# A new order of the small work around the scan steps of a Mamba layer: places by half step, delta and its product by channel half

## The chip, the cores and the metric

The kernel runs on one core of one Trainium2 chip. The metric is the device time of one execution in microseconds, the median of several runs. Work is spread over TensorE (PE), VectorE (DVE), ScalarE (ACT), GpSimd (POOL) and the DMA queue that SyncE (SP) feeds.

## The reference

An input of 4 x 128 x 128 x 128 (batch, channels, height, width) passes two layers. Layer 0 is a Mamba block over windows of 8 x 8 pixels:

```
tn  = layernorm over channels of the window's 64 tokens
xi, z = tn @ W_in                  (256 channels each)
xc  = silu(causal conv of xi over 4 taps + conv_b)
dr, Bm, Cm = xc @ W_x              (8, 16, 16 columns)
delta = softplus(dr @ dt_w + dt_b)
h_t = exp(delta_t * A) * h_(t-1) + (delta_t * xc_t) * B_t      for 16 states
y   = sum over states of h * C + xc * D,   then y * silu(z)
out = y @ W_out + b_out + x
```

Layer 1 normalises over channels, multiplies 16 filters in the frequency domain, mixes channels, applies a two-layer perceptron and adds its input. The change does not touch layer 1.

## The kernel before

**Blocks and steps.** Layer 0 is cut into 64 blocks of 16 windows (1024 tokens). A block is 32 steps (NSTEP): step n scans state n % 16 for half of the tokens (n < 16 the first 512, then the others), on all 256 channels held as 128 partitions x 2 halves. Every engine has one instruction stream, and `body(S, p)` of each engine writes it out step by step. `slots` runs the bodies: while block m is scanned (S.scan), the same 32 steps carry the front of block m+1 (S.front: projections, convolution, silu, delta), the layer norm of block m+2 (S.ahead), the output projection of block m-1 (S.back) and its spectra (S.tail). The engines are coupled by semaphores alone.

**One scan step.** In an even step (DSTEPS) the decay exp(delta*A) is written by ScalarE into the one PSUM buffer decay_d (`make_decay`, L734), and the drive delta*x*B is made by GpSimd (`make_drive`, L1020) from b_all, a row of B spread over the partitions by a DMA. In an odd step (RSTEPS) the decay goes to one of two SBUF buffers decay_r (L734), and the drive is made on ScalarE in token order (`scale_u`, L747, from ut and bt) and turned by TensorE into the one PSUM buffer drive_r (`turn_drive`, L591: 8 transposes). VectorE scans (L911, 32 a block). The product with C is made either by GpSimd (BY_GPSIMD: 20 of the 32 steps, L1031, with c_all from a DMA) or by VectorE (the 12 others, L922, with C spread by TensorE into PSUM, `broadcast_c`, L582). Three steps later TensorE adds the product into y_acc (`add_state`, L604: 8 transposes). Rings: 4 states, 4 products, 4 drives, 4 b_all, 4 c_all, one decay_d, one drive_r.

**Small work.** All other matrix work is a list of jobs, JOBS: (step, name, kind, bank). They share two PSUM banks, job_bank[0] and [1]; bank 0 also takes `broadcast_c`. A job waits until the job before it in its bank was read ("taken"), and a job in bank 0 waits also for the products of VectorE of all earlier steps. The names: z00 to z11 and conv00 to conv11 (channel half, token half), xp (the rows dr, B, C), dt (delta), bt and ut (B and delta*x turned to token order), turn (y turned back), out, mean, var, fy. The table AT says in which step the reader takes each result: `take_z` and `take_conv` (L771), `take_rows` (L754, L755), `take_dt`, `softplus`, `silu` and `copy_y` (L820) on ScalarE, `take_low` (L940), `take_ut` (L945), `gate` (L951), x1 (L967), stats (L973), mean_var (L977) on VectorE, `add_soft` (L1038), `make_du` (L1044), tn (L1069), edge (L1074) on GpSimd. A step has one place for this work on each engine: before `add_state` on TensorE, at the end of the step on the others. A convolution is already two half jobs, one step apart. `silu` costs two loads of activation tables besides its two activations.

**SyncE.** Its stream issues the loads of b_all 8 steps and of c_all 6 steps ahead, each after a wait on GpSimd that the buffer is free (L518, L524), and the loads and stores of x_in, x_res, x1 and the row spectra z (L566). All run on one queue in program order, and a wait holds back all that is behind it.

Of the kernel before, what the change touches and what calls it, by code (L numbers as in the profile page):

```python
# [63 lines left out]
BY_GPSIMD = tuple(sorted(RSTEPS + (2, 14, 18, 30)))  # L64
# [4 lines left out]

JOBS = [  # L70
# [14 lines left out]
]  # L85
SKIP_AT = {4: 0, 6: 1, 13: 2, 15: 3, 19: 0, 23: 1, 27: 2, 31: 3}
ADD_FIRST = (2, 18)
# [3 lines left out]
    "copy_y": (18, 2), "take_rows": (17, 0), "take_conv": (3, 8, 10, 12), "take_z": (0, 2, 8, 14),  # L91
# [2 lines left out]

# [2 lines left out]

# [1 line left out]

    "x_in": 15, "rows": (18, 1), "rows_landed": (24, 8), "x1_out": 18, "x_res": 23, "yo_out": 30,  # L100
}

# [28 lines left out]
class Slot:  # L131
# [14 lines left out]
    def at(self, n):  # L146
        return [j[1] for j in self.mine if j[0] == n]

    def jobs_below(self, bank, n):
        return self.start[bank] + sum(j[3] == bank and j[0] < n for j in self.mine)  # L150
# [263 lines left out]
def layer0(nc, a, wt, rows_dram, x1_dram, y_dram, blocks):  # L414
    with ExitStack() as ctx:
# [87 lines left out]
        def _(sp):  # L503
# [28 lines left out]
            def body(S, p):  # L532
# [3 lines left out]
                for n in range(NSTEP):  # L536
# [10 lines left out]
                    for k in range(NSTEP):  # L547
                        if k in DSTEPS and (k - B_LOAD) % NSTEP == n and S.step(n + B_LOAD, p):
                            load_b(S.step(n + B_LOAD, p))
                        if k in BY_GPSIMD and (k - C_LOAD) % NSTEP == n and S.step(n + C_LOAD, p):  # L550
                            load_c(S.step(n + C_LOAD, p))
                    if n == AT["x_in"] and S.ahead:
                        if S.front:
                            full(sp, S, "z11")
                        load_x(x_in, after, s["x_ready"])
                    if n == AT["x1_out"] and S.back:
                        need(sp, s["stats_done"], m)
                        sp.dma_start(x1_dram[bass.ds((m - 1) * WS, WS)].rearrange("r w c -> w r c"),
                                     x1[:]).then_inc(s["x1_stored"], 16)
# [4 lines left out]
                    if n == AT["yo_out"] and S.tail:  # L564
                        need(sp, s["yo_done"], m - 1)
                        sp.dma_start(yv[bass.ds(behind[1], 1), bass.ds(behind[0], 1)]  # L566
                                     .rearrange("o q f r d -> (o q f) r d"), yo[:]).then_inc(s["yo_stored"], 16)
# [8 lines left out]
        def _(pe):  # L576
            def broadcast_c(S, step):
# [3 lines left out]
                need(pe, job_taken[0], S.jobs_below(0, n + 1))  # L581
# [33 lines left out]
            def job(S, p, n, name, part=0):  # L615
# [50 lines left out]
                elif kind == "ut":  # L666
                    h, q = int(name[-2]), int(name[-1])
                    need(pe, s["du_done"], (m if q else m + 1) * 2 + q + 1)
                    for g in range(2):
                        for hf in range(2):  # L670
                            mm = pe.matmul(misc[:, (g * 2 + hf) * P:(g * 2 + hf + 1) * P],
                                           du[:, hf, q * HT + (2 * h + g) * P:q * HT + (2 * h + g + 1) * P],
                                           wt["ident"][:], start=True, stop=True, is_transpose=True)
# [19 lines left out]
                elif kind == "fy":  # L693
                    q = int(name[-1])
                    need(pe, s["z1_done"], (m - 2) * 2 + q + 1)
                    mm = pe.matmul(misc[:], wt["fy"][:], z1[:, 4 * q:4 * q + 4, :].rearrange("p r c -> p (r c)"),
                                   start=True, stop=True)
                if kind != "conv" or part == 1:
                    mm.then_inc(job_full[S.bank[name]], 1)

            def body(S, p):
                for n in range(NSTEP):
# [4 lines left out]
                    if n in ADD_FIRST and S.step(n - ADD_BEHIND, p):  # L707
                        add_state(S.step(n - ADD_BEHIND, p))
                    for name in S.at(n):
                        job(S, p, n, name)  # L710
# [884 lines left out]
```

## Time and profile before

| | |
|---|---|
| time, median of 3 runs (lowest, highest) | 9848.84 us (9843.6, 9866.34) |
| the profiled execution: time, span | 9848.94 us, 9847.1 us |
| busy share PE, DVE, ACT, POOL | 89%, 85%, 78%, 82% |
| granted TensorE clock, mean | 0.976 |
| bytes moved, share of 16 DMA engines | 934 MB, 30% |

The page shows layer 0 in the first 29 of its 40 slices: all four engines at seven to eight tenths, none at nine. In the rest, layer 1, TensorE is the busy engine. Two neighbouring records of one engine can overlap a little (the end of one is written back while the next one runs), so the time that an instruction takes in its stream is the distance between two starts.

### The profile page before, as it was taken

To read this page: it belongs to the slowest core of one execution; us is meant where nothing else is said; L and a number is where in the kernel's file an instruction comes from. 1 tells how busy PE (TensorE), PEld (TensorE's weight loads), DVE (VectorE), ACT (ScalarE), POOL (GpSimd) and SP (SyncE) were. 2 spreads that over 40 slices of the span, in tenths; PEclk is the share of its full clock that TensorE was granted. 3 is DMA by queue.
4 is the path that set the end of the run, shared out by engine and by line. 5 is a ranking of instruction groups with operands and counts; after the bars stand their busy time and mean duration, and the time that the engine had idled before them with its cause. 6 is when DMAs were issued, how large, how long until landed. Compare 5 with 4: busy or idle time off the path is not lost. (4 is left out here: it accounts for less than half of the span.)

```text
span 9847.1 us, 180628 instructions
## 1 busy us (share of the span) xinstructions
PE 8760.4 (89%) x54525; PEld 6830.6 (69%) x54525; DVE 8340.0 (85%) x8144; ACT 7719.1 (78%) x13926; POOL 8030.5 (82%) x3609
## 2 busy tenths in 40 slices
PE   7888888888889988888888888888799999999899
PEld 4666666666666666666666666666588888888788
DVE  5888888888888888888888888888788888888766
ACT  6888888888888888888888888888755555555577
POOL 5888888888888888888888888888788888888600
PEclk8999999999999999999999999999899999999999
DMA  3333333333333333333333333333300101010255
GB/s 90 107 110 104 109 106 113 104 110 107 112 106 107 104 112 105 110 104 114 104 110 104 115 102 110 104 114 103 104 31 31 35 31 35 31 35 31 67 186 179
DMA packets 648651, 933.96 MB, mean 95 GB/s; under 512 B 79960, under 2 KB 277600, under 8 KB 643552
## 3 DMA queue, kind: packets, MB, share of 16 engines
q1 hardware_dynamic: 647904, 924.64, 29.9%
q8 instruction: 391, 6.41, 0.3%
q14 instruction: 356, 2.92, 0.1%
HBM read 778.38 MB, written 146.04 MB: 94 GB/s over the span
## 5 line engine op out<-in xcount | busy, mean ns | idle before, releaser
L1031 POOL TENSOR_TENSOR prod<-state,c_all 128x1024 f32<-128x1024 f32 x1280 | 3021.1, 2365 | 495.5 <-DVE state L911 486.3
L911 DVE TENSOR_TENSOR_SCAN state<-decay_d,drive_d 128x1024 f32<-128x1024 f32 x1024 | 2338.3, 2283 | 353.7 <-ACT decay_d L734 351.6
L604 PEld LDWEIGHTS y_acc<-ident,prod 128*128 128x128 f32 x16384 | 1926.3, 144 | 839.2 <-issue 679.1
L1020 POOL TENSOR_TENSOR drive_d<-du,b_all 128x1024 f32<-128x1024 f32 x1024 | 2425.8, 2369 | 0.0
L911 DVE TENSOR_TENSOR_SCAN state<-decay_r,drive_r 128x1024 f32<-128x1024 f32 x1024 | 2327.9, 2273 | 100.3 <-PE drive_r L591 95.7
L604 PE MATMUL y_acc<-ident,prod 128*128 128x128 f32 x16384 | 2193.0, 279 | 94.5 <-ACT y_tok L820 91.7
L1312 DVE SCALAR_TENSOR_TENSOR sum_d<-bank_d,filt,sum_d 128x512 f32<-128x512 f32 x2470 | 1679.6, 744 | 265.0 <-PE bank_d L1220 238.9
L747 ACT ACTIVATE ub<-ut,bt 128x256 f32<-128x256 f32 x4096 | 1739.5, 499 | 37.4 <-issue 19.1
L1359 POOL TENSOR_TENSOR sum_p<-sum_p,scaled 128x1024 f32<-128x1024 f32 x650 | 1550.9, 2386 | 258.7 <-ACT scaled L1270 226.7
L1270 ACT ACTIVATE scaled<-bank_p,filt 128x512 f32<-128x512 f32 x1560 | 944.0, 688 | 734.0 <-PE bank_p L1220 659.4
L591 PE MATMUL drive_r<-ident,ub 128*128 128x128 f32 x8192 | 1114.3, 280 | 330.1 <-DVE state L911 185.6
L734 ACT ACTIVATE decay_d<-delta,neg_a 128x504 f32<-128x504 f32 x2048 | 1311.3, 674 | 89.0 <-DVE state L911 87.7
L734 ACT ACTIVATE decay_r<-delta,neg_a 128x504 f32<-128x504 f32 x2048 | 1343.6, 705 | 0.0
L591 PEld LDWEIGHTS drive_r<-ident,ub 128*128 128x128 f32 x8192 | 946.0, 145 | 388.1 <-issue 228.8
L922 DVE TENSOR_TENSOR prod<-state,job_bank 128x1024 f32<-128x1024 f32 x768 | 925.7, 1205 | 273.4 <-PE job_bank L582 253.7
L641 PE MATMUL job_bank<-x_in,tap_w 128*128 128x512 f32 (+3 forms) x2048 | 953.3, 593 | 2.3 <-ACT xc L771 2.3
L1220 PE MATMUL bank_d<-th_high,x_high 128*128 128x256 f32 x2600 | 791.1, 304 | 6.3 <-DVE x_low L1322 2.5
L1220 PE MATMUL bank_d<-th_high,x_low 128*128 128x256 f32 x2600 | 733.9, 282 | 0.0
L1220 PE MATMUL bank_d<-th_low,x_high 128*128 128x256 f32 x2600 | 733.7, 282 | 0.0
L641 PEld LDWEIGHTS job_bank<-x_in,tap_w 128*128 128x128 f32 x2048 | 363.5, 190 | 382.6 <-issue 377.4
L582 PE MATMUL job_bank<-c_rows,pick 48*128 48x512 f32 x768 | 381.1, 496 | 210.7 <-DVE ut L945 97.7
L1220 PE MATMUL bank_p<-th_high,x_high 128*128 128x256 f32 x1560 | 473.2, 303 | 57.0 <-ACT scaled L1270 57.0
(155 smaller groups left out, 14642.5 us busy)
## 6 DMA issues: line engine op xcount, KB each, us to landing
c_all<-bc_rows SPq DMA_DIRECT2D x1280, 256.0 KB, 3.3
b_all<-bc_rows SPq DMA_DIRECT2D x1024, 256.0 KB, 3.7
ys<-row_spectra SPq DMA_DIRECT2D x130, 256.0 KB, 2.8
column_sums<-tt SPq DMA_DIRECT2D x130, 256.0 KB, 2.1
x_in<-in_x_dram SPq DMA_DIRECT2D x64, 512.0 KB, 4.5
x_res<-in_x_dram SPq DMA_DIRECT2D x64, 512.0 KB, 4.6
x_rows<-x SPq DMA_DIRECT2D x64, 512.0 KB, 4.5
row_spectra<-z SPq DMA_DIRECT2D x64, 512.0 KB, 4.7
```

The source lines that it names most:

```text
L591: mm = pe.matmul(drive_r[:, hf, g * P:(g + 1) * P], ub[place_of(RSTEPS, n, NS_UB)][:, g, hf * P:(hf + 1) * P], wt["ident"][:], start=True, ...
L604: mm = pe.matmul(y_acc[:, g, hf * P:(hf + 1) * P], prod[n % NP][:, hf, g * P:(g + 1) * P], wt["ident"][:], start=(n % NS == 0 and hf == 0 ...
L641: mm = pe.matmul(o[:, :, k:WT], wt["tap_w"][:, K - 1 - k, hf * P:(hf + 1) * P], v[:, :, 0:WT - k], start=(k == 0), stop=(k == K - 1), skip ...
L734: last = act.activation(dst[:, hf, :, 1:WT], delta[:, hf, q * HT:(q + 1) * HT].rearrange("p (w t) -> p w t", t=WT)[:, :, 1:WT], ACT.Exp, s ...
L747: last = act.activation(ub[place_of(RSTEPS, n, NS_UB)][:, g, :], ut[q][:, g, :], ACT.Copy, scale=bt[q][:, g, st:st + 1])
L911: dve.tensor_tensor_scan(state[n % NT][:].rearrange("p h t -> p (h t)"), decay[:].rearrange("p h w t -> p (h w t)"), drive[:].rearrange("p ...
L1020: pool.tensor_tensor(drive_d[place_of(DSTEPS, n, ND)][:], du[:, :, q * HT:(q + 1) * HT], b_all[slot][:].unsqueeze(1).to_broadcast([P, 2, HT]),
L1031: pool.tensor_tensor(prod[n % NP][:], state[n % NT][:], c_all[slot][:].unsqueeze(1).to_broadcast([P, 2, HT]), ALU.mult).then_inc(s["prod_g ...
L1220: mm = pe.matmul(o, x[p][:, part, b, :], th[:, 2 * pair:2 * pair + 2, :].rearrange("p l h -> p (l h)"), start=(b % 2 == 0 and i == 0), sto ...
L1270: act.activation(scaled[n % 2][:, i, out, :].rearrange("p (b h) -> p b h", b=B), bank_p[:, :, i, :], ACT.Copy, scale=filt[p][:, kind, 2 * ...
L1312: dve.scalar_tensor_tensor(acc, src, factor, acc, ALU.mult, ALU.add).then_inc(s["summed_d"], 1)
L1359: pool.tensor_tensor(acc, acc, scaled[n % 2][:, i], ALU.add).then_inc(s["summed_p"], 1)
```

## The change

It gives each step two places for the small work, before and after the step's main instructions, and rewrites the tables: JOBS and AT now count half steps (0 to 63; h is in step h // 2). Further: which four even steps' products GpSimd makes; delta and du on GpSimd, and ut on TensorE and VectorE, by channel half instead of whole (ut was by token half); z1 in four pieces instead of two; the statistics in two; the silu stands ahead of the decays of step 17 instead of behind those of step 15; SyncE's stores and x loads stand ahead of a step's b and c loads, and the store of spectra at step 26 instead of 30. The second half of a convolution follows two half steps after the first, which is one step as before.

```diff
-BY_GPSIMD = tuple(sorted(RSTEPS + (2, 14, 18, 30)))
+BY_GPSIMD = tuple(sorted(RSTEPS + (8, 12, 18, 20)))
 JOBS = [
-    (0, "z00", "front", 0), (0, "xp1", "scan", 1),
-    (2, "z10", "front", 0), (2, "conv00", "front", 1),
-    (4, "turn10", "back", 0), (4, "dt01", "scan", 1), (5, "dt11", "scan", 1),
-    (6, "turn11", "back", 0), (6, "bt1", "scan", 1), (7, "conv10", "front", 1),
-    (8, "z01", "front", 0), (9, "conv01", "front", 1),
-    (10, "ut01", "scan", 0), (11, "conv11", "front", 1),
-    (12, "ut11", "scan", 0), (13, "out0", "back", 1),
-    (14, "z11", "front", 0), (15, "out1", "back", 1),
-    (17, "xp0", "front", 1), (19, "dt00", "front", 1),
-    (20, "turn00", "scan", 0), (20, "dt10", "front", 1), (21, "mean0", "ahead", 1),
-    (22, "turn01", "scan", 0), (22, "mean1", "ahead", 1),
-    (24, "bt0", "front", 0), (24, "var0", "ahead", 1), (25, "var1", "ahead", 1),
-    (26, "ut00", "front", 0), (28, "ut10", "front", 0),
-    (28, "fy0", "tail", 1), (29, "fy1", "tail", 1),
+    (0, "z00", "front", 0), (0, "xp1", "scan", 1), (3, "conv00", "front", 1), (7, "z10", "front", 0),
+    (8, "turn10", "back", 0), (8, "dt01", "scan", 1), (10, "dt11", "scan", 1), (12, "bt1", "scan", 0),
+    (12, "conv10", "front", 1), (15, "turn11", "back", 0), (18, "z01", "front", 0), (18, "conv01", "front", 1),
+    (19, "ut01", "scan", 0), (22, "conv11", "front", 1), (24, "ut11", "scan", 0), (27, "z11", "front", 0),
+    (28, "out0", "back", 1), (31, "out1", "back", 1), (35, "xp0", "front", 1), (37, "turn00", "scan", 0),
+    (37, "dt00", "front", 1), (41, "dt10", "front", 1), (42, "mean0", "ahead", 0), (44, "mean1", "ahead", 0),
+    (48, "turn01", "scan", 0), (48, "var0", "ahead", 1), (49, "var1", "ahead", 1), (50, "ut00", "front", 1),
+    (51, "ut10", "front", 0), (51, "fy0", "tail", 1), (53, "bt0", "front", 0), (58, "fy1", "tail", 1),
 ]
-SKIP_AT = {4: 0, 6: 1, 13: 2, 15: 3, 19: 0, 23: 1, 27: 2, 31: 3}
-ADD_FIRST = (2, 18)
+CONV_GAP = 2
+SKIP_AT = {4: 0, 5: 1, 14: 2, 15: 3, 22: 1, 23: 0, 30: 2, 31: 3}
 AT = {
-    "copy_y": (18, 2), "take_rows": (17, 0), "take_conv": (3, 8, 10, 12), "take_z": (0, 2, 8, 14),
-    "take_dt0": (19, 20), "take_dt1": (4, 5), "softplus0": 21, "softplus1": 6, "silu": 15, "take_bt": (24, 6),
-    "square": (22, 23), "deviation": (24, 25), "less_mean": 22, "deviation1": 26, "z1": (1, 7), "yo": (28, 29),
-    "low": (18, 1), "take_ut0": (26, 28), "take_ut1": (10, 12),
-    "centre": (21, 23), "gate0": (20, 22), "gate1": (4, 6), "x1": (14, 16), "stats": 17, "mean_var": 19,
-    "delta0": 22, "delta1": 7, "du0": 23, "du1": 8, "edge": 13, "shift1": 27, "tn": (26, 27),
-    "x_in": 15, "rows": (18, 1), "rows_landed": (24, 8), "x1_out": 18, "x_res": 23, "yo_out": 30,
+    "copy_y": (35, 6), "take_rows": (35, 1), "take_conv": (7, 16, 21, 27), "take_z": (0, 7, 18, 30),
+    "softplus0": 43, "softplus1": 13, "silu": 34, "take_bt": (54, 13), "square": (45, 48), "deviation": (47, 50),
+    "less_mean": 52, "deviation1": 55, "z1": (3, 5, 19, 21), "yo": (52, 59),
+    "low": (37, 2), "take_dt0": (40, 42), "take_dt1": (10, 11), "take_ut0": (51, 52), "take_ut1": (19, 25),
+    "centre": (43, 45), "gate0": (38, 49), "gate1": (9, 15), "x1": (30, 33), "stats": (30, 34), "mean_var": 43,
+    "delta0": (43, 45), "delta1": (15, 15), "du0": (46, 48), "du1": (15, 21), "edge": 27, "shift1": 63,
+    "tn": (56, 60),
+    "x_in": 15, "rows": (17, 0), "rows_landed": (24, 6), "x1_out": 16, "x_res": 25, "yo_out": 26,
 }
...
+            def jobs(S, p, h):
+                for name in S.at(h):
+                    job(S, p, h // 2, name)
+                for name in S.at(h - CONV_GAP):
+                    if name.startswith("conv"):
+                        job(S, p, h // 2, name, 1)
 
             def body(S, p):
...
-                    for name in S.at(n):
-                        job(S, p, n, name)
-                    for name in S.at(n - 1):
-                        if name.startswith("conv"):
-                            job(S, p, n, name, 1)
-                    if n not in ADD_FIRST and S.step(n - ADD_BEHIND, p):
+                    jobs(S, p, 2 * n)
+                    if S.step(n - ADD_BEHIND, p):
                         add_state(S.step(n - ADD_BEHIND, p))
                     if n in SKIP_AT and S.scan:
-                        add_skip(p, n // NS, SKIP_AT[n])
+                        add_skip(p, (n - ADD_BEHIND) // NS, SKIP_AT[n])
+                    jobs(S, p, 2 * n + 1)
```

On ScalarE and GpSimd `others(S, p, 2n)` stands ahead of the step's decays, drives and products and `others(S, p, 2n + 1)` behind them. On VectorE the order is scan, `others(2n)`, product, `others(2n + 1)`. The new `add_soft`, for one:

```diff
-            def add_soft(M, q):
+            def add_soft(M, q, hf):
                 need(pool, s["softplus_done"], M * 4 + 2 * q + 2)
-                d = delta[:, :, q * HT:(q + 1) * HT]
-                pool.tensor_tensor(d, d, soft[:], ALU.add).then_inc(s["delta_done"], 1)
+                d = delta[:, hf, q * HT:(q + 1) * HT]
+                pool.tensor_tensor(d, d, soft[:, hf, :], ALU.add).then_inc(s["delta_done"], 1)
```

## Rows read from the trace of the kernel before

**Rows 1.** Windows: one block of the first layer, then sixty blocks.

```profile
2362.66:2471.98 109.32, 95.94 (x586) 70.81 (x585) 95.63 (x75) 96.86 (x180) 96.36 (x44) 0.98 0.35 108
391.97:6960.69 6568.72, 5797.19 (x35041) 4271.79 (x35039) 5740.12 (x4442) 5807.84 (x10741) 5782.09 (x2640) 0.98 0.34 108
```

**Rows 2.** What VectorE waited for in that one block: total, times, longest.

```profile
DVE state L911 <- ACT decay_d L734: 6.3, 4, 3.2
DVE prod L922 <- PE job_bank L582: 3.4, 2, 1.8
DVE state L911 <- PE drive_r L591: 1.4, 2, 0.8
DVE ut L945 <- PE job_bank L671: 1.3, 2, 0.7
DVE gated L951 <- PE job_bank L679: 1.0, 1, 1.0
```

**Rows 3.** Timeline of VectorE in that block: start, us, what, idle before.

```profile
2362.66 0.62 DVE L977 BATCH_NORM_AGGREGATE mv<-stats 128x2 f32<-128x6 f32 x8
...
2399.73 2.27 DVE L911 TENSOR_TENSOR_SCAN state<-decay_d,drive_d 128x1024 f32<-128x1024 f32 x1
2401.91 2.26 DVE L911 TENSOR_TENSOR_SCAN state<-decay_r,drive_r 128x1024 f32<-128x1024 f32 x1
2405.96 1.22 DVE L922 TENSOR_TENSOR prod<-state,job_bank 128x1024 f32<-128x1024 f32 x1 [1.79 <-PE job_bank L582]
...
2415.61 2.29 DVE L911 TENSOR_TENSOR_SCAN state<-decay_d,drive_d 128x1024 f32<-128x1024 f32 x1 [3.22 <-ACT decay_d L734]
...
2466.74 2.29 DVE L911 TENSOR_TENSOR_SCAN state<-decay_d,drive_d 128x1024 f32<-128x1024 f32 x1 [2.05 <-ACT decay_d L734]
...
2471.98 0.61 DVE L977 BATCH_NORM_AGGREGATE mv<-stats 128x2 f32<-128x6 f32 x8
```

**Rows 4.** Timeline of ScalarE in that block.

```profile
2409.68 1.65 ACT L838 ACTIVATE z<-x,shift,rstd 128x128 f32<-128x128 f32 x4 [1.88 <-DMA row_spectra<-z]
...
2454.30 0.69 ACT L771 ACTIVATE zs<-job_bank,z_b 128x512 f32<-128x512 f32 x1 [2.06 <-PE job_bank L646]
...
2457.42 1.28 ACT L796 ACT_TABLE_LOAD   x1
...
2463.74 1.70 ACT L747 ACTIVATE ub<-ut,bt 128x256 f32<-128x256 f32 x4
2465.35 1.27 ACT L734 ACTIVATE decay_d<-delta,neg_a 128x504 f32<-128x504 f32 x2
```

**Rows 5.** Timeline of TensorE in that block.

```profile
2399.95 1.09 PE L591 MATMUL drive_r<-ident,ub 128*128 128x128 f32 x8 [2.21 <-DVE state L911]
...
2426.55 1.97 PE L641 MATMUL job_bank<-x_in,tap_w 128*128 128x512 f32 x4
2428.36 1.04 PE L604 MATMUL y_acc<-ident,prod 128*128 128x128 f32 x8
2429.23 1.04 PE L591 MATMUL drive_r<-ident,ub 128*128 128x128 f32 x8
...
2471.46 1.97 PE L604 MATMUL y_acc<-ident,prod 128*128 128x128 f32 x8 [0.53 <-ACT y_tok L820]
```

**Rows 6.** Groups of GpSimd instructions in that block: busy, mean ns, idle before.

```profile
L1031 POOL TENSOR_TENSOR prod<-state,c_all 128x1024 f32<-128x1024 f32 x20 | 47.1, 2358 | 7.8 <-DVE state L911 7.5
...
L1038 POOL TENSOR_TENSOR delta<-delta,soft 128x1024 f32<-128x1024 f32 x2 | 4.7, 2374 | 3.4 <-ACT soft L792 3.4
...
L1069 POOL TENSOR_TENSOR x_in<-cent,sq 128x512 f32<-128x512 f32 x2 | 2.5, 1264 | 0.0
```

**Rows 7.** Timeline of SyncE's queue: the store of row spectra.

```profile
2404.91 0.40 SPq L566 DMA_DIRECT2D row_spectra<-z  x1
```

**Rows 8.** The page's DMA issues: kind, count, KB each, us to landing.

```profile
b_all<-bc_rows SPq DMA_DIRECT2D x1024, 256.0 KB, 3.7
...
row_spectra<-z SPq DMA_DIRECT2D x64, 512.0 KB, 4.7
```

More of the change, by code:

```diff
@@ L144, in __init__, with at, jobs_below @@
         self.size = [sum(j[3] == bank for j in self.mine) for bank in range(2)]
[L146 to L150, printed above, removed]
+    def at(self, h):
+        return [j[1] for j in self.mine if j[0] == h]
+    def jobs_below(self, bank, h):
+        return self.start[bank] + sum(j[3] == bank and j[0] < h for j in self.mine)
     def step(self, n, p):
@@ L563, in body @@
                         load_x(x_res, now, s["xres_ready"])
[L564 to L567, printed above, removed]
+                    for k in range(NSTEP):
+                        if k in DSTEPS and (k - B_LOAD) % NSTEP == n and S.step(n + B_LOAD, p):
+                            load_b(S.step(n + B_LOAD, p))
+                        if k in BY_GPSIMD and (k - C_LOAD) % NSTEP == n and S.step(n + C_LOAD, p):
+                            load_c(S.step(n + C_LOAD, p))
             sp.sem_inc(s["x1_stored"], 16)
@@ L857, in body @@
+                    if (n + 2) % NSTEP in RSTEPS and S.step(n + 2, p):
+                        make_decay(S.step(n + 2, p))
                     if (n + 3) % NSTEP in RSTEPS and S.step(n + 3, p):
@@ new lines, in statistics, with mean_var, others @@
+            def statistics(S, q):
+                taken(dve, S, f"out{q}")
+                for r in range(4 * q, 4 * q + 4):
+                    last = dve.bn_stats(stats[:, r, :], x1[:, r, :])
+                last.then_inc(s["stats_done"], 1)
+            def mean_var():
+                for r in range(WS):
+                    last = dve.bn_aggr(mv[:, r, :], stats[:, r, :])
+                last.then_inc(s["mv_done"], 1)
+            def others(S, p, h):
+                m, f = S.m, 1 - p
+                if h == AT["low"][1] and S.scan:
+                    take_low(S, m, 1)
+                if h == AT["low"][0] and S.front:
+                    take_low(S, m + 1, 0)
+                for hf in range(2):
+                    if h == AT["take_ut1"][hf] and S.scan:
+                        take_ut(S, hf, 1)
+                    if h == AT["take_ut0"][hf] and S.front:
+                        take_ut(S, hf, 0)
+                    if h == AT["gate0"][hf] and S.scan:
+                        gate(S, 0, hf, p)
+                    if h == AT["gate1"][hf] and S.back:
+                        gate(S, 1, hf, f)
+                for q in range(2):
+                    if h == AT["centre"][q] and S.ahead:
+                        centre(S, q)
+                    if h == AT["x1"][q] and S.back:
+                        take_x1(S, q)
+                    if h == AT["stats"][q] and S.back:
+                        statistics(S, q)
+                if h == AT["mean_var"] and S.back:
+                    mean_var()
@@ L998, in body @@
-                    if S.scan and n in AT["gate0"]:
-                        gate(S, 0, AT["gate0"].index(n), p)
-                    if S.ahead:
-                        ahead(S, n, m)
-                    if S.back:
-                        behind(S, n, m, f)
+                    others(S, p, 2 * n + 1)
             dve.memset(decay_d[:].rearrange("p i w t -> p (i w t)"), 0.0)
@@ new lines, in add_edge, with others @@
+            def add_edge(S, f):
+                taken(pool, S, "conv00", "conv10", "conv01", "conv11")
+                v = xc[f][:].rearrange("p k (w t) -> p k t w", t=WT)[:, :, 0:K - 1, :]
+                pool.tensor_tensor(v, v, wt["edge"][:].unsqueeze(3).to_broadcast([P, 2, K - 1, NW]),
+                                   ALU.add).then_inc(s["edge_done"], 1)
+            def others(S, p, h):
+                m, f = S.m, 1 - p
+                for hf in range(2):
+                    if h == AT["delta1"][hf] and S.scan:
+                        add_soft(m, 1, hf)
+                    if h == AT["du1"][hf] and S.scan:
+                        make_du(m, 1, hf, p)
+                    if h == AT["delta0"][hf] and S.front:
+                        add_soft(m + 1, 0, hf)
+                    if h == AT["du0"][hf] and S.front:
+                        make_du(m + 1, 0, hf, f)
+                if h == AT["shift1"] and S.back:
+                    make_shift1(m)
+                for q in range(2):
+                    if h == AT["tn"][q] and S.ahead:
+                        make_tn(S, q)
+                if h == AT["edge"] and S.front:
+                    add_edge(S, f)
```

313 lines of the change are left out of this document (139 added, 174 removed).

## The prediction

> **What bounds the kernel now.** I read the page first, then cut layer 0 by windows. A clean block lasts 109.3 us, sixty together 6568.7, so 109.5 each, and in the clean one VectorE, ScalarE and GpSimd are busy 95.6, 96.9 and 96.4 us [rows 1]. None of them is full: each idles some 13 us of a block, and TensorE's records cover about as much. The block is set by four streams that wait for each other in turn. VectorE is the one to follow, since every scan runs there and the state goes from there to all the others. Its waits are listed next: 6.3 + 3.4 + 1.4 + 1.3 + 1.0 = 13.4 us a block, by what ended them [rows 2]. The reader should see that 95.6 + 13.4 is the block; this sum is what the change can move, since it removes no scan and no product. The timeline then says where they lie [rows 3]: 1.79 and 3.22 us at the start of a block (steps 1 and 4), 2.05 at step 18 behind the silu. The rest: about 1.75 for drives and a decay ahead of that (steps 15 to 17), 1.0 for a turned y (step 20), and 3.6 in steps 7 to 12, where products, a decay and ut come late behind convolutions. Layer 1 and the setup stay as they are.
>
> **The change, part by part.** Its order can be walked through for one block: every instruction starts at the later of its engine's end of work and what it waits for. Distances between starts, from rows: a scan 2.2 (2399.73 to 2401.91) [rows 3]; silu with its tables 6.3 (2457.42 to 2463.74), scale_u 1.6 (to 2465.35), a decay 1.2, a copy from a bank 0.6 [rows 4]; the first half of a convolution 1.8, eight transposes 0.87, a job of two matmuls half a convolution's first half, 0.86 [rows 5]; a product on GpSimd 2.33 [rows 6]; a product on VectorE 1.1 (its record, 1.22, overlaps the next a little) [rows 3]. For a signal between engines I take 0.15 to 0.2. Zero is the end of the scan of step 31.
>
> *Silu.* Before, ScalarE stood 2.06 us before z11 just ahead of the decay of step 16 [rows 4], then ran the silu, then scale_u 19, then decay 18. Now z11 is made at h27 and read at h30, 1 to 2 us after it is there, and scale_u 19 goes ahead of the silu. From the end of scan 14, decay 18 is ready after 0.2 + 1.2 + 1.2 + 1.6 + 6.3 + 1.2 = 11.7. VectorE needs until then three scans (6.6), two products (2.2), two x1 (1.2) and two half statistics (1.7), 11.7, and waits 0.25 for out1 and 0.3 for drive 17. Loss 0.55, where it was 3.8, and the 1.0 for the turned y is gone: turn00 is ready 2 us early. Silu is hidden behind this work of VectorE alone; without it, it costs what stands in excess, as the 2.05 did.
>
> *Start of a block.* Before, z00 was read behind the rows of xp1, so C could not be spread (1.79), and ScalarE stood 1.88 us for the store of the spectra and then had z1, two reads and copy_y ahead of decay 4 (3.22) [rows 3, 4]. Now z00 is read first, z1 comes in two pieces behind the decays, and the store is issued earlier. Walk: 0.2 for the rows' high part, 0.5 for C of step 2 behind the second half of conv00, 0.05 for decay 4. Loss 0.75 for 5.0.
>
> *Steps 4 to 9.* TensorE from its start of step 4 (14.5) to turn11: two drives 1.7, four add_state 3.5, three short turns and skips of 0.44 with one more 1.8, two dt 1.7, bt 0.9, two C 0.9, two halves of conv10 3.5, which is 13.9 and 0.5 of waits. So turn11 is ready at 29.0 and its gate ends at 29.75, while VectorE had 12.2 of work from 13.55. It loses 0.8 (turn10, held until z10 is read), 1.35 (C of step 6 behind conv10), 1.85 (turn11); then 0.7 for ut01. Loss 4.7 for 3.6: this stretch gets worse.
>
> *Steps 20 to 26.* dt10 and softplus0 stand around decay 22: losses 0.65, 0.5 and 0.15, 1.3, where there was none.
>
> *Delta and du in halves.* GpSimd's 128 x 512 product takes 1.26, the whole 2.37 [rows 6]: four times 1.26 for 2.37 twice over, 4 x (2 x 1.26 - 2.37) / 2 = 0.3 for delta and as much for du in a block, 0.6 together if no half is cheaper (bounds 0, two halves of 1.19, and 0.6); I take 0.6. GpSimd then stands 2.8 for softplus0 and runs without a gap to the block's end; the product of step 23 is ready about 1 us ahead of scan 27, so the 0.6 lies beside scans. With that cover gone it costs its 0.6.
>
> *Edge and ut with other strides; z1 and statistics in pieces.* No row shows these strides. Edge is 96 elements a partition, and the longest row for so few would be that of half a product, so its price is between nothing and 1.26 [rows 6]; the silu asks for it some 2 us later, which hides it. The ut copy is as many elements as before, 0.68; between 0 and doubled, 2.7 a block; I take 0, as its rows stay 128 elements long.
>
> *SyncE.* The store of spectra stands at step 26 but waits for a read that ScalarE does at h59, step 29. Behind it wait the b loads of steps 2 and 4 and the c loads of 1 and 3 of the next block. In the walk it goes out at 97.2 and takes 0.4 to issue [rows 7]; b of step 2 follows and lands after 3.7, or, queued behind the store's 4.7, after 8.4 [rows 8]: 101.7 to 106.4. GpSimd asks for it at 103.7, and scan 2 needs the drive at 109. With the drive's 2.33 the bad end gives 108.7, so it costs nothing at either end, with 0.3 us to spare. The waits at steps 16 and 12 to 15 (statistics at step 17; c_all of neighbouring products) leave 1 to 3 us.
>
> *Sum.* 0.55 + 0.75 + 4.7 + 1.3 = 7.3 us of idle for 13.4. Add 0.7, because eight transposes behind a wait took 1.09 and not 0.87 on three or four of those hand-overs [rows 5]: 8.0. A block comes to 109.3 - 5.4 = 103.9, times 64 blocks 346 us. From the profiled execution's 9848.9, which equals the median: 9503.
>
> **Rivals.**
> *A, the forecast:* 9503, own range 9430 to 9590 (a block between 102.8 and 105.3).
>
> *B, TensorE at half clock where it is needed.* Behind a wait at 2471.46 eight transposes took 1.97, double the 1.04 [rows 5], and the granted clock over sixty blocks was 0.98 [rows 1]. In the walk TensorE idles 1.1 to 1.6 us around the block's start and in steps 18 and 23, and steps 0 to 9 have no room. Two such stretches a block, each with two sets of eight transposes (0.9 more for a set, 1.7 in all), give 3.4 us: a gain of 2.0 a block, 9721. Against: it waited 2.21 us at the block's start before [rows 5], and the clock hardly fell. (TensorE: Matmul & The Clock Gate, "What's actually happening", of the Trainium skill has it that the half rate is the resting state and only activity releases it; the doubled row agrees.)
>
> *C, GpSimd is the bound.* It is as busy as any of the three [rows 1], the change takes nothing from it and adds 0.6 a block: 38 us, 9887. Against: it waits 7.8 + 3.4 us a block for states and the softplus [rows 6]. [...]
>
> *D, SyncE's store.* If b of step 2 lands 9 us after the store's issue or later, each us more moves scan 2. It is slower than before from 5.4 us beyond that; at 7 beyond, the block is 110.9 and the time 9950. Nothing in the rows lands so late [rows 8].
>
> *E, the walk is too harsh:* halves of stalls in steps 4 to 9 gone because ScalarE runs ahead: 102.2 a block, 9395.
>
> *F, no change that can be measured:* losses elsewhere eat the gain; a block of 109.3.
>
> **Chances.** A 0.56, B 0.18, E 0.08, D 0.04, C 0.04, F 0.04, small gains between B and F 0.06. The range from 9400 to 9730 leaves out half of E, C, D, F and part of the small gains, near 0.2. Under 0.2% (20 us) a measurement of this kernel can't tell from no change; faster by more 0.88, within 0.04, slower 0.08.
>
> **What would show it.** The block falls to near 104 us with VectorE's busy time the same 95.6. Its wait for decay_d falls from 6.3 to about 1.5 us a block, that for C from 3.4 to about 2, that for turned y rises from 1.0 to about 2.6. ScalarE no longer waits for the spectra's DMA, nor 2 us for z11. GpSimd has 44 + 4 instructions a block, and its busy time is 97. B would show as a granted clock under 0.96 in layer 0; D as GpSimd's drive waiting for a DMA; C as GpSimd at 98% of the block. The prediction is wrong if a wait that the walk has at zero, the drive of step 17 or a c_all load, turns up with a microsecond or more in each block.

## The result, and the profile after

| | before | after |
|---|---|---|
| time, median (lowest, highest), us | 9848.83 (9843.6, 9866.34) | 9546.7 (9528.44, 9548.83) |
| profiled execution: time, span | 9848.94, 9847.1 | 9544.83, 9543.0 |

The ratio of the times is 0.9688, with an interval from 0.9676 to 0.9699. The change takes 302 us off; forecast were 346, and 9503 lies 44 us (0.5%) below the median measured. Now the page of the changed kernel: busy times, the two groups that are to be looked at, and the two kinds of DMA issue that answer to [rows 8].

```profile
PE 8679.4 (91%) x54525; PEld 6752.8 (71%) x54525; DVE 8330.0 (87%) x8144; ACT 7711.4 (81%) x13926; POOL 8059.3 (84%) x3865
...
L919 DVE TENSOR_TENSOR_SCAN state<-decay_d,drive_d 128x1024 f32<-128x1024 f32 x1024 | 2337.2, 2282 | 158.0 <-issue 86.0
L1034 POOL TENSOR_TENSOR drive_d<-du,b_all 128x1024 f32<-128x1024 f32 x1024 | 2422.9, 2366 | 53.0 <-DMA b_all<-bc_rows 48.9
...
b_all<-bc_rows SPq DMA_DIRECT2D x1024, 256.0 KB, 3.8
...
row_spectra<-z SPq DMA_DIRECT2D x64, 512.0 KB, 3.7
```

The busy times hardly differ from before (TensorE's by 1%, the others' by 30 us or less); the shares rise because the span fell. The second line has something new: of the 158.0 us that stand before the even scans, 86.0 are put down to "issue", time in which VectorE waited for nothing that the trace shows. The third says that GpSimd waited 48.9 us for loads of b_all.

A block is again measured from one mean_var on VectorE (the first of eight L980) to the next. Windows of two blocks in a row, and of 59 together (columns as in [rows 1]):

```profile
2899.40:3001.69 102.29, 94.67 (x587) 69.33 (x586) 95.49 (x76) 96.63 (x180) 96.22 (x48) 1.00 0.36 114
3001.69:3108.98 107.29, 95.97 (x586) 70.39 (x585) 95.46 (x76) 96.63 (x180) 97.23 (x50) 0.98 0.35 112
381.40:6565.12 6183.72, 5633.29 (x34459) 4128.19 (x34458) 5634.52 (x4367) 5703.31 (x10562) 5711.40 (x2832) 0.99 0.36 113
```

59 blocks make 6183.72, a mean of 104.8 for the 109.5 of before, and 4.7 x 64 is about the 302 us. But there is no block of 104.8: they alternate between 102.3 (four of these 103.5) and a longer one, 103.8 to 109.1, on average 107.3. The loop of the program covers two blocks in one turn, and a block that holds the jump back to its start is the long one. Before, blocks with the jump lasted 109.5 on average and those without it 109.4.

**The short block** first. What VectorE waited for in it, which answers to [rows 2]:

```profile
DVE gated L956 <- PE job_bank L677: 2.7, 2, 1.9
DVE prod L930 <- PE job_bank L582: 1.7, 2, 1.4
DVE state L919 <- ACT decay_d L734: 1.0, 3, 0.4
DVE ut L950 <- PE job_bank L670: 0.6, 1, 0.6
DVE state L919 <- PE drive_r L591: 0.3, 1, 0.3
DVE x L968 <- PE job_bank L689: 0.3, 1, 0.3
```

These sum to 6.6 us where [rows 2] had 13.4. The timeline of VectorE in that block says which they are (it answers to [rows 3]):

```profile
2900.46 2.29 DVE L919 TENSOR_TENSOR_SCAN state<-decay_d,drive_d 128x1024 f32<-128x1024 f32 x1 [0.43 <-ACT decay_d L734]
...
2907.03 2.29 DVE L919 TENSOR_TENSOR_SCAN state<-decay_d,drive_d 128x1024 f32<-128x1024 f32 x1 [0.40 <-ACT decay_d L734]
...
2942.20 1.22 DVE L930 TENSOR_TENSOR prod<-state,job_bank 128x1024 f32<-128x1024 f32 x1 [0.26 <-PE job_bank L582]
...
2946.38 0.69 DVE L956 TENSOR_TENSOR gated<-job_bank,zs 128x512 f32<-128x512 f32 x1 [0.76 <-PE job_bank L677]
...
2956.30 1.22 DVE L930 TENSOR_TENSOR prod<-state,job_bank 128x1024 f32<-128x1024 f32 x1 [1.45 <-PE job_bank L582]
...
2959.46 0.69 DVE L956 TENSOR_TENSOR gated<-job_bank,zs 128x512 f32<-128x512 f32 x1 [1.94 <-PE job_bank L677]
...
2965.08 0.69 DVE L950 COPY ut<-job_bank 128x512 f32<-128x512 f32 x1 [0.56 <-PE job_bank L670]
...
2985.80 0.69 DVE L968 TENSOR_TENSOR x<-job_bank,out_b_rows 128x512 f32<-128x512 f32 x1 [0.27 <-PE job_bank L689]
2986.83 2.29 DVE L919 TENSOR_TENSOR_SCAN state<-decay_r,drive_r 128x1024 f32<-128x1024 f32 x1 [0.34 <-PE drive_r L591]
```

The reader can lay this beside the walk: decay 22 and 24, C of step 2, turn10, C of step 6, turn11, ut01, out1, drive 17, one after the other. GpSimd in the same window (answers to [rows 6]):

```profile
L1045 POOL TENSOR_TENSOR prod<-state,c_all 128x1024 f32<-128x1024 f32 x20 | 47.3, 2371 | 0.9 <-DVE state L919 0.9
...
L1058 POOL TENSOR_TENSOR du<-delta,xc 128x512 f32<-128x512 f32 x4 | 5.1, 1276 | 0.2 <-POOL delta L1052 0.2
L1052 POOL TENSOR_TENSOR delta<-delta,soft 128x512 f32<-128x512 f32 x4 | 5.1, 1275 | 4.6 <-ACT soft L791 4.6
...
L1076 POOL TENSOR_TENSOR xc<-xc,edge 128x96 f32<-128x96 f32 x1 | 0.4, 430 | 0.0
```

Its wait for states fell from 7.5 to 0.9: it follows the scans almost without a gap.

**The long block.** The jump falls between steps 31 and 0. Timelines of TensorE, VectorE, ScalarE, SyncE's queue and GpSimd around it:

```profile
3031.36 0.61 PE L612 MATMUL y_acc<-diag_d,xc 128*128 128x128 f32 x4
3036.17 1.96 PE L591 MATMUL drive_r<-ident,ub 128*128 128x128 f32 x8 [4.20 <-issue]
...
3032.23 1.20 DVE L930 TENSOR_TENSOR prod<-state,job_bank 128x1024 f32<-128x1024 f32 x1
3036.19 2.29 DVE L919 TENSOR_TENSOR_SCAN state<-decay_d,drive_d 128x1024 f32<-128x1024 f32 x1 [2.77 <-issue]
...
3043.01 0.68 DVE L945 TENSOR_TENSOR c_rows<-job_bank,c_rows 16x512 fp32r<-16x512 f32 x1 [2.35 <-ACT c_rows L755]
...
3039.73 0.69 ACT L770 ACTIVATE zs<-job_bank,z_b 128x512 f32<-128x512 f32 x1 [7.03 <-PE job_bank L646]
...
3028.20 0.40 SPq L549 DMA_DIRECT2D row_spectra<-z  x1
3028.71 0.51 SPq L518 DMA_DIRECT2D b_all<-bc_rows  x1
...
3035.68 2.35 POOL L1034 TENSOR_TENSOR drive_d<-du,b_all 128x1024 f32<-128x1024 f32 x1 [1.34 <-DMA b_all<-bc_rows]
```

TensorE stands 4.20 us and VectorE 2.77 with no releaser; both resume within 0.02 us of each other, which is chance: at the 29 jumps of the loop VectorE's first scan starts between 0.6 us before and 1.2 us after TensorE's first transposes. VectorE then waits 2.35 more for c_rows, because ScalarE reads z00 first, and TensorE was late with it. 2.77 + 2.35 is the 5 us. Over the 29 jumps TensorE stands 2.1 to 5.0 us (median 4.0) and VectorE 1.8 to 3.95. Windows of 4 us over the same place (last three columns: granted clock, DMA share, GB/s):

```profile
3028.00:3032.00 4.00, 3.48 (x26) 2.88 (x25) 4.00 (x2) 3.54 (x7) 4.00 (x4) 1.00 0.67 163
3032.00:3036.00 4.00, 0.00 (x0) 0.00 (x0) 1.42 (x2) 0.71 (x2) 2.66 (x3) 1.00 0.98 287
3036.00:3040.00 4.00, 3.83 (x12) 2.56 (x13) 3.81 (x2) 0.27 (x1) 4.00 (x3) 0.57 0.25 91
```

In the middle one the DMA engines are full (0.98): the store of spectra and the loads behind it. The kernel before, TensorE and VectorE at one of its back edges:

```profile
2287.90 0.61 PE L612 MATMUL y_acc<-diag_d,xc 128*128 128x128 f32 x4
2291.45 1.09 PE L591 MATMUL drive_r<-ident,ub 128*128 128x128 f32 x8 [2.94 <-DVE state L911]
...
2288.32 2.26 DVE L911 TENSOR_TENSOR_SCAN state<-decay_r,drive_r 128x1024 f32<-128x1024 f32 x1
2290.50 2.26 DVE L911 TENSOR_TENSOR_SCAN state<-decay_d,drive_d 128x1024 f32<-128x1024 f32 x1
```

There VectorE's scans follow each other 2.18 us apart, with a jump or without. The row puts TensorE's 2.94 down to a state, but the state explains only part of it: where no jump falls, TensorE waits 2.21 at this place [rows 5] and starts 0.12 behind the state, at all 29 places; with the jump it waits 2.5 to 3.8 (median 2.94). At six jumps of 29 the trace finds no releaser (3.5 to 3.8), and those six blocks last 109.4 to 111.7 where the other 23 with a jump last 109.3 on average. So the jump held TensorE 0.3 to 1.6 us longer before too; in the blocks it hardly showed.

What runs in the stop is in the DMA view, as packets of the kind "instruction". The stop of TensorE above (3031.97 to 3036.17), then that of the kernel before (2288.51 to 2291.45), columns as in the page's third part (packets, MB, share of 16 engines):

```profile
q8 instruction: 1, 0.02, 1.5%
q14 instruction: 2, 0.02, 1.0%
```
```profile
q8 instruction: 1, 0.02, 2.5%
q14 instruction: 2, 0.02, 1.4%
```

The packet of q8, 16 KB, starts at 3033.45 and takes 1.00 us, and TensorE starts 1.72 us after its end. The same distance stands at every jump: 1.56 to 1.79 us at the 29 of the changed kernel, 1.57 to 1.82 at the 29 of the kernel before, however long the stop. Where no jump falls there is no such link (in the kernel before, 3.1 to 5.8 us since the last packet of q8).

### The profile page after: what moved, and what is told of

It is laid out like the page before. It is cut to its first block and busy times, and to the rows that moved or that the text cites. A ratio compares the mean times of both kernels' runs of the same rounds, so it can differ in the third digit from the quotient of the medians.

```text
span 9543.0 us, 181899 instructions
## 1 busy us (share of the span) xinstructions
PE 8679.4 (91%) x54525; PEld 6752.8 (71%) x54525; DVE 8330.0 (87%) x8144; ACT 7711.4 (81%) x13926; POOL 8059.3 (84%) x3865
## 5 line engine op out<-in xcount | busy, mean ns | idle before, releaser
L919 DVE TENSOR_TENSOR_SCAN state<-decay_d,drive_d 128x1024 f32<-128x1024 f32 x1024 | 2337.2, 2282 | 158.0 <-issue 86.0
L1034 POOL TENSOR_TENSOR drive_d<-du,b_all 128x1024 f32<-128x1024 f32 x1024 | 2422.9, 2366 | 53.0 <-DMA b_all<-bc_rows 48.9
L604 PEld LDWEIGHTS y_acc<-ident,prod 128*128 128x128 f32 x16384 | 1861.5, 141 | 627.8 <-issue 532.5
L604 PE MATMUL y_acc<-ident,prod 128*128 128x128 f32 x16384 | 2152.3, 275 | 40.6 <-POOL prod L1045 36.8
L1052 POOL TENSOR_TENSOR delta<-delta,soft 128x512 f32<-128x512 f32 x256 | 326.8, 1277 | 288.6 <-ACT soft L791 288.6
```

Of the source, the lines that this page charges most:

```text
L604: mm = pe.matmul(y_acc[:, g, hf * P:(hf + 1) * P], prod[n % NP][:, hf, g * P:(g + 1) * P], wt["ident"][:], start=(n % NS == 0 and hf == 0 ...
L919: dve.tensor_tensor_scan(state[n % NT][:].rearrange("p h t -> p (h t)"), decay[:].rearrange("p h w t -> p (h w t)"), drive[:].rearrange("p ...
L1034: pool.tensor_tensor(drive_d[place_of(DSTEPS, n, ND)][:], du[:, :, q * HT:(q + 1) * HT], b_all[slot][:].unsqueeze(1).to_broadcast([P, 2, HT]),
```

## The experiments

In all of them the kernel edited is the changed one, unless the name says before. "Block" means the distances from mean_var to mean_var. The kernel before, run beside them, gave 9849.73, 9853.67 and 9848.51 us.

**The store of spectra back at step 30** (`e1_store30`).

```diff
-    ..., "x_res": 25, "yo_out": 26,
+    ..., "x_res": 25, "yo_out": 30,
```

> The changed kernel with one number put back: the store of the row spectra stands at SyncE's step 30 again, not 26. Theory 1 (the store's early wait dams up the loads of b and c, they go out together at the end of a block, and at the loop's back edge, every second block, TensorE and VectorE stand until that burst is through): the long blocks fall from 107.3 us to near the short ones' 102.3, VectorE's wait with no releaser at the edge from 2.8 us to under 0.5, so about 31 x 5 = 155 us less, 9390. Rival 2 (the stop belongs to the back edge itself and was hidden before by TensorE's idle time there): the blocks stay 102.3 and 107.3, time 9547 within 15. Rival 3 (z1 then waits for the later store, as before the change): all blocks rise by 1 to 3 us, 9600 or more.

Measured: 9492.07 us (9476.92 to 9517.49), ratio 0.9632 [0.9615, 0.9648], 55 us less. The stall stays and gets smaller: blocks with the jump 105.2 to 107.7, for the most part 106.0 to 106.2, TensorE idle 2.1 to 3.7 us at an edge (median 3.25), VectorE 1.8 to 2.5. The time lies between theory 1 and rival 2 and in the range of neither. A row of VectorE's timeline at one edge, and the page's line for GpSimd's drives:

```profile
2398.29 2.29 DVE L919 TENSOR_TENSOR_SCAN state<-decay_d,drive_d 128x1024 f32<-128x1024 f32 x1 [2.50 <-issue]
```
```profile
L1034 POOL TENSOR_TENSOR drive_d<-du,b_all 128x1024 f32<-128x1024 f32 x1024 | 2422.5, 2366 | 11.1 <-DMA b_all<-bc_rows 9.9
```

So the burst of transfers behind the store is 1.0 (means) to 1.5 (medians) of the 5 us; the rest is there without it. That makes 30 to 45 us. The profiled executions differ by 27 us (spans 9515.7 and 9543.0), the medians by 55; where the rest of the 55 lies is not shown.

**A loop turn of four blocks** (`e2_four_blocks`).

```diff
-    with eng.Fori(0, (blocks - 4) // 2) as j:
-        for i in range(2):
+    with eng.Fori(0, (blocks - 4) // 4) as j:
+        for i in range(4):
...
```

> The changed kernel with four blocks in a turn of the loop instead of two; instructions and their order are the same otherwise. If the long blocks belong to the back edge (with or without the burst), only every fourth block is long: 16 fewer long blocks at 5 us, 80 us less, 9467. If they belong to what the two parities of blocks do (other buffers, other rows), every second block stays long and the time is 9547 within 15.

Measured: 9455.69 us (9451.91 to 9469.23), ratio 0.9604 [0.9588, 0.962]. Now only every fourth block is long (104.6 to 107.7), the other three last 102.1 to 102.3 (three blocks 103.2). The excess goes with the jump and with nothing in a block's own work.

**The silu three half steps earlier** (`e3_silu31`).

```diff
-"silu": 34
+"silu": 31
```

> The changed kernel with the silu at half step 31, behind the decays of step 15 and ahead of scale_u 19 as in the kernel before. Theory A (by the walk, decay 18 is ready at the same time either way and what helped was that z11 is long made): short blocks stay within 0.7 us of 102.3, time 9547 within 40; TensorE waits near 2 us for ub of step 19 again. Rival (the silu's place behind scale_u 19 brought the gain of that stretch, 3 us a block): short blocks at 105, time near 9740.

Measured: 9524.84 us (9501.28 to 9544.07), ratio 0.9662 [0.9645, 0.9679], its profiled span 9542.2 beside 9543.0. Short blocks 102.3 as before the edit. The wait of TensorE for scaled rows that was expected did not show. The runs spread over 43 us, so the 22 between the medians say little. Where the silu stands within these three half steps does not matter; the likely reason, not tried apart, is that the product and x1 of VectorE cover it at either place.

**The kernel before with its store at step 26** (`b1_store26`).

```diff
-    ..., "yo_out": 30,
+    ..., "yo_out": 26,
```

> The kernel before the change with only the store of the row spectra moved from SyncE's step 30 to 26. If the burst of loads stops the engines at the back edge whatever the order of work, every second block grows from 109.4 to 112 or more, 9930 or above. If it costs only where TensorE has no idle time to hide it, the time stays at 9849 within 20; if the store mattered for z1 alone, the wait of 1.9 us goes from every block and the time falls by up to 100 us.

Measured: 9831.48 us (9824.64 to 9840.82), ratio 0.998 [0.9971, 0.999]. ScalarE's wait for the spectra's DMA is gone, but the jump's stall now shows here too (TensorE 3.1 to 3.35 without a releaser at 28 jumps of 29, VectorE 0.2 to 1.5 us), and blocks come out between 106.5 and 111.6. The earlier store alone is worth 18 us here.

**The old choice of GpSimd's even products** (`e4_old_products`).

```diff
-BY_GPSIMD = tuple(sorted(RSTEPS + (8, 12, 18, 20)))
+BY_GPSIMD = tuple(sorted(RSTEPS + (2, 14, 18, 30)))
```

> The changed kernel with the products of steps 2, 14, 18 and 30 on GpSimd again, as in the kernel before, in place of 8, 12, 18 and 20. Theory (places in the table were cut to the products: jobs in bank 0 now stand where no product of VectorE is under way): C of steps 8, 12 and 20 holds z01, z11 and mean0, blocks grow by 1 to 4 us; but VectorE's last instruction before the back edge is a scan again, so its wait with no releaser goes from 2.8 us to under 0.5 at each edge and some 2 of the 5 us come back. In sum between 9500 and 9700. Rival (which steps' products go to GpSimd makes no difference inside a block): short blocks 102.3, edges shorter, 9480.

Measured: 10158.11 us (10121.32 to 10169.33), ratio 1.0299 [1.0272, 1.0325]: 611 us slower than the changed kernel and slower than the one before. Theory and rival both missed it: blocks last 112 to 117, so they grew by 10 to 15 us where the theory had 1 to 4. In a block of 116.0 us, VectorE's waits and TensorE's:

```profile
DVE ut L950 <- PE job_bank L670: 7.4, 2, 6.9
DVE cent L936 <- PE job_bank L627: 3.4, 3, 1.3
```
```profile
PE job_bank L646 <- DVE prod L930: 4.6, 2, 4.2
```

A job in bank 0 may not start before VectorE has read C of all earlier steps. The new JOBS puts z01 (h18) and ut01 (h19) into that bank right behind step 8, whose product then is VectorE's; z01 waits 4.2 us for it and ut01 6.9 behind it. VectorE's stall at the jump is gone in this kernel, as its last instruction is then a scan; TensorE still stands 2.7 to 2.8 us without a releaser at most jumps.

**Delta and du whole again** (`e5_whole_delta`). Both halves are made at the place of the first; `make_du` is edited in the same way.

```diff
-                d = delta[:, hf, q * HT:(q + 1) * HT]
-                pool.tensor_tensor(d, d, soft[:, hf, :], ALU.add).then_inc(s["delta_done"], 1)
+                if hf == 1:
+                    return
+                d = delta[:, :, q * HT:(q + 1) * HT]
+                pool.tensor_tensor(d, d, soft[:], ALU.add).then_inc(s["delta_done"], 2)
```

> The changed kernel with delta and delta*x made whole on GpSimd (one instruction of 128 x 1024 at the place of the first half), all else kept. By the prediction the halves cost GpSimd 0.6 us a block that no scan waits for: 44 GpSimd instructions a block, GpSimd busy near 95.7, short blocks 102.3, time 9547 within 20. Rival (the halves let ut start sooner and so carry part of the gain): VectorE's wait for ut01 grows by 1 us or more, or decay 0 and drive 0 come late, blocks grow by 0.5 to 2 us, 9580 to 9670.

Measured: 9524.37 us (9517.12 to 9529.7), ratio 0.9664 [0.9648, 0.968], 22 us less, 3 us outside the expected range, and the two kernels' runs overlap by 1 us (9529.7 and 9528.44). Short blocks are 102.3 as before, and none is 103.5 any more; blocks with the jump last 106.6 on average for 107.3. So most of what shows with the loop lies in the long blocks.

**One product moved, 20 for 30** (`e6_product30`).

```diff
-BY_GPSIMD = tuple(sorted(RSTEPS + (8, 12, 18, 20)))
+BY_GPSIMD = tuple(sorted(RSTEPS + (8, 12, 18, 30)))
```

> The changed kernel with one product put back: step 30's on GpSimd (it is VectorE's last instruction before the loop's back edge), step 20's on VectorE. Theory (each engine needs 3 to 4 us from the last instruction it could send until the first behind the back edge, and VectorE's product of step 30 makes that moment late): VectorE's wait with no releaser at the edge falls under 1.5 us; TensorE's stays, since its last instruction is unmoved. Long blocks fall by 1 to 2.5 us, short ones may grow by up to 1: 9480 to 9540. Rival (VectorE stands because TensorE's first drive is late): long blocks unchanged, 9547 or more.

Measured: 9725.11 us (9718.98 to 9726.46), ratio 0.9867 [0.9851, 0.9884], 178 us slower than the changed kernel, where theory had 9480 to 9540. The part on VectorE came true: it has no unexplained stop at the edges any more, so it is the product of step 30, its last instruction ahead of the jump, that lays the jump bare. TensorE still stands 2.7 us at two edges of three. But product 20 is now VectorE's, and mean0 (h42, bank 0) waits for it. VectorE's timeline there:

```profile
2432.01 0.69 DVE L936 TENSOR_TENSOR cent<-x_in,job_bank 128x512 f32<-128x512 f32 x1 [1.70 <-PE job_bank L627]
```

TensorE had waited 2.1 us there for VectorE's product. Nearly all blocks come to 106 to 109, with a jump or without: those without grew by about 6 us, where up to 1 was expected.

**The loop written out, changed kernel and kernel before** (`e7_no_loop`, `b2_no_loop`).

```diff
-    with eng.Fori(0, (blocks - 4) // 2) as j:
-        for i in range(2):
-            body(Slot(j * 2 + 2 + i, ...), i)
+    for m in range(2, blocks - 2):
+        body(Slot(m, ...), m % 2)
```

> The changed kernel with the loop written out: 60 blocks in a row, no back edge, the same instructions in the same order. If the long blocks are the back edge's, all blocks are 102.3 and the time is 9547 - 30 x 5 = 9395 within 25. If every second block stays near 107, the edge is innocent. If instructions come too slowly when none is repeated, waits with no releaser appear everywhere and the time is above 9547.

> The kernel before the change with its loop written out, no back edge. Theory (in that order of work TensorE stands 2 us at a block's start anyway and VectorE's last instruction is a scan sent early, so the back edge was hidden): blocks stay near 109.3, time 9849 within 25. Rival (each back edge cost 4 to 5 us in both kernels): 120 to 150 us less.

Measured: e7 9409.59 us (9406.7 to 9412.75), ratio 0.9548 [0.9532, 0.9564]; b2 9854.58 (9840.63 to 9864.94), ratio 1.0006 [0.9996, 1.0015]. In e7 blocks last 102.2, about every fifth 103.4, and none is long. The same jump is worth 137 us in one kernel and nothing in the other.

**z00 read behind the rows again** (`e9_z00_behind_rows`).

```diff
-"take_z": (0, 7, 18, 30)
+"take_z": (1, 7, 18, 30)
```

> The changed kernel with z00 read behind the rows of xp1, as in the kernel before, instead of ahead of them. The prediction put the product's wait of 1.8 us at a block's start down to this order: then C of step 0 comes later by the two reads, about 1 us more wait for that product, 50 to 70 us in all, 9600. Rival (by the walk, rows come 0.6 us sooner when they go first, which gives the same back at the rows' low part): blocks within 0.3 us of before, 9547 within 20.

Measured: 9570.31 us (9537.48 to 9600.72), ratio 0.9707 [0.9687, 0.9726], its profiled span 9598.9; short blocks last 102.7 or 103.9, on average 0.9 more than the changed kernel's. The profiled execution, the slowest of the four, so agrees with the theory's number, and the median is 24 us above the changed kernel's, under half of it. The runs spread over 63 us. The sign is that of the theory; the size is not settled.

**z11 made one step later** (`e10_z11_late`).

```diff
-(27, "z11", "front", 0)
+(29, "z11", "front", 0)
```

> The changed kernel with the job z11 moved from half step 27 to 29, behind out0, so that ScalarE waits for it ahead of the decay of step 16 and then of the silu, as in the kernel before. Theory (z11 made early is what keeps the silu off the scans): ScalarE waits 4 us there, the decays of steps 16 and 18 come late, a block grows by 3 to 4.5 us, 9740 to 9830. Rival (VectorE has slack of several us there): within 60 us of 9547.

Measured: 9824.47 us (9798.54 to 9831.27), ratio 0.9971 [0.9961, 0.998]: 278 of the 302 us are lost by this one number. Half of the blocks without a jump last 106.3, 4.0 more, the others 107.7 to 108.8. In a block of 106.3, waits of ScalarE and of VectorE:

```profile
ACT zs L770 <- PE job_bank L646: 6.8, 3, 3.7
```
```profile
DVE state L919 <- ACT decay_d L734: 3.2, 4, 2.2
DVE prod L930 <- PE job_bank L582: 2.8, 3, 1.5
```

ScalarE stands before z11 again, and what its stream has behind reaches VectorE late: the wait for decays is 3.2 for 1.0, that for C 2.8 for 1.7.

**Loop written out, delta and du whole** (`e11_no_loop_whole`): the edits of e7 and e5 together.

> The changed kernel with the loop written out and delta and delta*x whole: the two edits that each took time off. The halves of delta gave 22 us with the loop; if that came from the long blocks alone (GpSimd gets through the end of a block sooner), nothing is left of it here: 9410 within 10. If it came from every block, 9388.

Measured: 9391.27 us (9388.63 to 9396.11), ratio 0.9536 [0.952, 0.9552], the fastest of all, 155 us below the changed kernel and 18 below e7. All blocks last 102.2; the windows row of one:

```profile
2219.68:2321.86 102.18, 94.72 (x587) 69.22 (x585) 95.35 (x75) 96.61 (x180) 95.50 (x44) 1.00 0.38 116
```

## Why the prediction was right, and where it was off

**Silu, start of a block, steps 4 to 9, steps 20 to 26: right, wait by wait.** Forecast and measured: decay 22 0.65 and 0.43, decay 24 0.5 and 0.40, decay 26 0.15 and 0.16; rows' low part 0.2 and 0; C of step 2 0.5 and 0.26; decay 4 0.05 and 0; turn10 0.8 and 0.76; C of step 6 1.35 and 1.45; turn11 1.85 and 1.94; ut01 0.7 and 0.56; out1 0.25 and 0.27; drive 17 0.3 and 0.34. The losses come to 6.6 for 7.3, and those of steps 4 to 9, the stretch that was to get worse, to 4.7 for 4.7. The 0.7 for restarts of the transposes was not needed. The short block is so 102.3 instead of 103.9. That z11 in time carries the silu's part was forecast, and e10 shows it; e3 shows that the silu's own place has slack. That the start of the block hangs on z00's place has e9's sign for it, not its size. e4 and e6 add what the walk had used without pricing: the choice of products and the JOBS table are one change. The table without its products costs 611 us (e4), with one of them exchanged 178 (e6), as bank 0 couples them.

**The sum: the mechanism right, the count of blocks not.** The walk took all 64 blocks for alike, as they had been. 7.2 us x 64 would have been 461, to 9388; e7, the same kernel without the jump, ran at 9410, and e11, without the halves too, at 9391. The changed kernel loses 5.0 us in each of the loop's 30 turns, 150 us, and 461 - 150 = 311 is what was found within 9. The mis-sized term is the block's 103.9: it was 1.6 too long, and the jump's 5.0 in every second one was missing. The two errors went opposite ways, and that is luck: it is why the total missed by only 44 us. Had the jump cost nothing, the time would have been that of e7, below the forecast's own range of 9430 to 9590 and just inside the wider one, 9400 to 9730. Rival E's time, 9395, is the one that the loop-free kernels meet, though not for E's reason.

**The jump had been hidden, not free.** b2 shows that it cost the kernel before nothing that can be measured (the six longer blocks are 7 us in all), e2 and e7 that it costs the changed one: 91 us for 15 turns fewer, 137 for all 30. The cover that went was idle time. Before, TensorE had 2.21 us to wait for a state at that place in any case, and VectorE had two scans to run, so the 0.3 to 1.6 us that the jump added on TensorE reached VectorE at few jumps. TensorE's last four matmuls started 0.42 us ahead of scan 31 then and start 1.31 behind it after, and VectorE's last instruction is a product where it was that scan. e6 shows the part of that product: with a scan as its last instruction, VectorE no longer stops. What TensorE stands for is the fetch of its code: the 16 KB packet of kind "instruction" in each stop, after whose end TensorE starts with a constant distance (1.56 to 1.82 us at 58 jumps of two kernels). That q8 carries TensorE's code is inferred from this distance. For VectorE no packet has such a fixed distance to its restart, so there the fetch is argued. (Runtime: NRT & Kernel Launch, "Instruction fetch mechanics", of the Trainium skill says that a taken branch to code outside the prefetched pages makes the engine fetch it by DMA before it goes on. The trace agrees: the packet took 1.00 us in a stop of 4.20.)

**SyncE: "it costs nothing at either end" was wrong, by 27 to 55 us.** b of step 2 landed 6.8 us after its issue, within the 3.7 to 8.4 of the walk, and GpSimd's drive of step 2 waited 1.34 without holding scan 2, which began only at 3044.86. So as rival D's late load it cost nothing. But it fills the DMA engines (0.98) just while the engines stand at the jump, and e1, which puts the store back, shortens the stop of TensorE by 0.7 us and that of VectorE by 0.9 (medians). The code packet itself takes as long in both kernels (0.98 and 0.97 us), but it starts 1.31 us after TensorE's last matmul, and 0.55 after it with the store put back. What delays its start is not shown. Full DMA engines alone do not: their share in the stop was 0.96 in the changed kernel and 0.49 in e1 (medians), but 0.89 in e6, whose stops last 2.8 us. In the kernel before, the earlier store was worth 18 us (b1).

**GpSimd's halves beside scans: nearly.** They add 0.7 us of work a block (4 x 1.275 + 4 x 1.276 for 4 x 2.37), forecast were 0.6; whole ones gain 22 us with the loop (e5) and 18 without (e11 beside e7), a third of a microsecond a block that the forecast had put at nothing. In e7 the cost sits in those blocks of 103.4, and they are gone in e11. The new strides cost nothing measurable: ut's copy is still 0.69, edge 0.43.

**The rivals.** B: TensorE's granted clock was 0.99 over 59 blocks; right behind a jump it was 0.57 in a window of 4 us, after TensorE had stood for 4.2, and eight transposes took 1.96 there. That is the half rate in one place of two blocks, part of the jump's price. C: GpSimd's wait for states, 0.9 us, shows that it is now close, but it does not set the block. D is told above. F: no. Of the signs named ahead, VectorE's busy time stayed (95.49), the wait for decay_d fell to 1.0 (forecast 1.5), that for C to 1.7 (2), that for the turned y rose to 2.7 (2.6), ScalarE's waits for the DMA and for z11 went (it waits 1.93 and 1.17 for two other z jobs instead), and GpSimd's 48 instructions took 96.2 us (97).

## What to carry to other kernels

When several engines wait for each other in turn and none is full, list the waits of the one that all depend on, walk the new order by hand with distances between starts from the trace, and sum what is left: here all twelve terms came out within 0.25 us. But a cost that was hidden in idle time (a loop's jump, a restart) has no row of its own in the waits of before, so ask of each wait that a change removes what else had been standing in it, and count blocks with and without the jump apart. If the unrolled program can be had, it is the cheap remedy: 137 us here, and nothing in the kernel whose waits covered the jump. A wait that the trace puts down to another engine can hide a fetch of code; the packets of kind "instruction" in that stretch tell.

## What the runs showed of the hardware

- A loop's back edge stops TensorE for 2.1 to 5.0 us and VectorE for 1.8 to 3.95 in the changed kernel, shown as idle time without a releaser; with four blocks a turn it comes half as often, and written out not at all.
- In each such stop of TensorE stands one 16 KB packet of queue q8, kind "instruction", of 0.9 to 1.2 us (in one of the 29 it begins just before); TensorE's first matmul follows its end by 1.56 to 1.79 us. In the kernel before the packet takes 0.9 to 2.15 us and the distance is 1.57 to 1.82, though the trace puts most of those waits down to a state.
- With the store of spectra at step 26 that packet starts 1.31 us after TensorE's last matmul, beside a DMA share of 0.96 in the stop; at step 30 it starts 0.55 after it, beside 0.49. It takes 0.98 and 0.97 us (medians). What delays its start is not shown.
- On GpSimd a product of half the elements takes 1.28 for 2.37 us: a fixed part of about 0.2 us each time it is cut.
